# Second layer of a graph network: two maxima of the next tile between the two weight products of this one, on Vector

## The chip, the cores and the metric

The kernel runs on one core of one Trainium2 chip. The metric is the time of one execution on the device, in microseconds; of several runs the median is given. The profile comes from one further execution.

## The reference

Two message-passing layers over 6250 nodes and 200000 edges, each with a residual and a layer norm. The change concerns the second layer only. For each edge e with 16 attributes and source node features h (16), it computes two 16 x 16 matrices and a softmax over the edges of a destination node:

```
w_m = (efeat @ W_msg + b_msg).reshape(E, 16, 16)
w_a = (efeat @ W_attn + b_attn).reshape(E, 16, 16)
e1 = w_m * feat[src][:, :, None]
e2 = w_a * feat[src][:, :, None]
seg_max = segment_max(e2, dst)
ex = exp(e2 - seg_max[dst])
attn = ex / segment_sum(ex, dst)[dst]
ft = segment_sum(e1 * attn, dst)
out = layernorm(x + x + ft.sum(axis=1))      # second x: the layer's input again
```

The last line is shortened to what matters: the layer adds its messages to its input and normalises.

## The kernel before, in words

The edges are sorted by destination. The first layer and all tables are made ahead, up to about 3000 us into the span; the second layer's loop over its edges follows, and a last block gathers the sums by node and normalises, from about 6095 us on. Only the loop is of interest here (kernel lines 1007 to 1298).

The loop runs over NT = 214 tiles. A tile is 128 partitions (lanes) times J = 8 edges, in two groups of G4 = 4; all edges of a group have the same destination. A lane walks along its sorted edges, so the running maximum and the running sums are carried from group to group and from tile to tile in the tiles `state` and `ps`. A device loop (`rounds`, L1024) has eight tiles in its body, since buffers rotate by tile number: `work`, `xg` and `state` have four buffers each, PSUM's `pw` has four banks.

In one step of the loop each engine works on the tile `now` and on its neighbours, in its own written order; semaphores join the engines.

- GpSimd gathers the source features of a later tile, eight indirect DMAs (L1082), and the edge rows of a still later one (L1091). The eight gathers wait until Vector has finished with the buffer.
- TensorE (L1152 on) sums the four edges of the previous tile's first group into PSUM (L1172, eight passes in f32), turns the edge rows of the next tile but one (L1195), waits for ScalarE's L1116 and for the second weight product, sums three edges of the second group (L1172), makes half of the difference of maxima (L1207, L1181), and makes the next tile's weights, 99 x 512 per edge (`weigh`, L1166), into `pw`.
- Vector (L1223 on) is where the change is. In a step it does, before the change: `maxima(now)`: two 512-wide maxima over pairs of edges, L1248 for the first group and L1250 for the second (each waits for ScalarE's masks, the semaphore `masked`), both into `top`; L1252, a maximum of these; three 256-wide scalar_tensor_tensor that carry the maximum from the tile before (L1254, L1258, L1261); two subtractions (L1266), one per group. Then the four L1235 of `edges(ahead)`: weights times source features, from `pw` into `work`, each of which waits for TensorE. Then L1281 of `carry_on(now)`, which scales the carried sums, and two products `products(now, half)` (L1273): exponentials times messages, one per group, each after ScalarE's exponential. Instructions that need the result of the one just before them on Vector wait for it through the semaphore `chain`; it rises by MS = 5 per tile.
- ScalarE (L1096 on) multiplies one edge's weights itself (L1109), fills and copies sums (L1116, L1117, L1148), turns rows to bf16 (L1123), takes two exponentials per tile (L1129), one of the difference (L1131), and masks the eight edges of the next tile (L1141), two after each of Vector's L1235.
- SP stores `state` for each tile (L1050, L1052) and loads the next metadata (L1040).

The order of each engine's work is the order in which these lines are written; no planner moves it.

The functions that the diff touches, and what calls them:

Of the kernel before, what the change touches and what calls it, by code (L numbers as in the profile page):

```python
# [52 lines left out]
C = D * D  # L53
# [42 lines left out]
def gnn(nc, x, src, dst, ea16, ea8, node_vec1, Wmt, Wml, Wut, Wul, Wm, bm, Wa, ba, out):  # L96
    ctx = ExitStack()
    with ctx:
# [96 lines left out]
        with ExitStack() as st:  # L195
            def tsb(name, shape, dt=F32):
                return st.enter_context(nc.sbuf_tensor(name, shape, dt))
# [16 lines left out]
            first = tsb("first", [PL, TN + 1])  # L214
# [748 lines left out]
        with ExitStack() as st:  # L963
# [8 lines left out]
            state = tsb("state", [GP, 4, 6 * C])  # L972
            top = tsb("top1", [GP, 7, C])
# [36 lines left out]
            def tile(t, q, off):  # L1010

                m = q + off
                if isinstance(t, int) and not 0 <= U * t + m < NT:
                    return None
                return U * t + m, m % U, t + m // U

            def channels(t, a=None):
                return t.rearrange("p (i o) -> p i o", i=D) if a is None else t.rearrange("p (i a o) -> p i a o", i=D, a=a)

            def wait(eng, what, value):  # L1020
                if not isinstance(value, int) or value > 0:
                    eng.wait_ge(what, value)

            def rounds(eng, body, before, after):  # L1024

                for n in range(-before, U):
                    body(n // U, n % U)
                with eng.Fori(1, NT // U) as t:
                    for q in range(U):
                        body(t, q)  # L1030
                for n in range(NT // U * U, NT + after):
                    body(n // U, n % U)

            def word(b, i):
                return mt[:, b, i:i + 1].bitcast(F32)
# [187 lines left out]
            @block.vector  # L1223
            def _(v):
                v.sem_inc(w_used, 2)
                v.tensor_scalar(nident[:, :], ident[:, :], -1.0, None, ALU.mult)
                v.wait_ge(primed, 1)
                v.wait_ge(ps_zeroed, 1)

                def edges(at, i):  # L1230

                    n, b, r = at
                    v.wait_ge(w_made, J * n + i + 2)
                    k = 1 if i == 2 else 2
                    v.tensor_tensor(work[:, b % 4, i:i + k, :, :, :].rearrange("p j i a o -> p (j i) (a o)"),  # L1235
                                    pw[:, i % 4:i % 4 + k, :].rearrange("p j (i c) -> p (j i) c", i=D),
                                    xg[:, b % 4, i:i + k, :].rearrange("p j i -> p (j i)").unsqueeze(2).to_broadcast([GP, k * D, 2 * D]),
                                    ALU.mult).then_inc(w_used, 1)

                def maxima(at):  # L1240

                    n, b, r = at
                    s = work[:, b % 4, :, :, 0, :]
                    out = lambda lo, hi: top[:, lo:hi, :].rearrange("p j (i o) -> p j i o", i=D)
                    both = top[:, 0:4, :].rearrange("p (g s) c -> p g s c", g=2)
                    before, first, second = state[:, (b - 1) % 4, C:2 * C], state[:, b % 4, 0:C], state[:, b % 4, C:2 * C]
                    v.wait_ge(masked, J * n + G4)
                    v.tensor_tensor(out(0, 2), s[:, 0:2], s[:, 2:4], ALU.max)  # L1248
                    v.wait_ge(masked, J * n + J)
                    v.tensor_tensor(out(2, 4), s[:, 4:6], s[:, 6:8], ALU.max).then_inc(chain, 1)  # L1250
                    v.wait_ge(chain, MS * n + 1)
                    v.tensor_tensor(top[:, 4:6, :], both[:, :, 0, :], both[:, :, 1, :], ALU.max).then_inc(chain, 1)  # L1252
                    v.wait_ge(chain, MS * n + 2)
                    v.scalar_tensor_tensor(out=top[:, 6, :], in0=before, scalar=word(b, FIRST_NEG),  # L1254
                                           in1=top[:, 4, :], op0=ALU.add, op1=ALU.max).then_inc(chain, 1)
                    wait(v, stored[b % 4], 32 * (2 * r + b // 4))
                    v.wait_ge(chain, MS * n + 3)
                    v.scalar_tensor_tensor(out=second, in0=top[:, 6, :], scalar=word(b, SECOND_NEG),  # L1258
                                           in1=top[:, 5, :], op0=ALU.add, op1=ALU.max).then_inc(chain, 1)
                    v.wait_ge(chain, MS * n + 4)  # L1260
                    v.scalar_tensor_tensor(out=first, in0=second, scalar=word(b, SECOND_NEG),  # L1261
                                           in1=top[:, 6, :], op0=ALU.add, op1=ALU.max).then_inc(chain, 1)
                    v.wait_ge(chain, MS * n + 5)
                    for half, most in enumerate((first, second)):
                        s = work[:, b % 4, half * H:(half + 1) * H, :, 0, :]
                        v.tensor_tensor(s, s, channels(most).unsqueeze(1).to_broadcast([GP, H, D, D]),  # L1266
                                        ALU.subtract).then_inc(less, 1)

                def products(at, half):
                    n, b, r = at  # L1270
                    v.wait_ge(exped, 2 * n + half + 1)
                    w = work[:, b % 4, half * H:(half + 1) * H, :, :, :]
                    v.tensor_tensor(w[:, :, :, 1, :], w[:, :, :, 1, :], w[:, :, :, 0, :], ALU.mult).then_inc(p_done, 2)  # L1273

                def carry_on(at):

                    n, b, r = at
                    v.wait_ge(corr_done, n + 1)
                    wait(v, b_summed, n)
                    wait(v, a_copied, n)  # L1280
                    v.tensor_tensor(channels(ps[:, 0, :], 2), channels(ps[:, 1, :], 2),  # L1281
                                    channels(corr[:, b % 4, :]).unsqueeze(2).to_broadcast([GP, D, 2, D]),
                                    ALU.mult).then_inc(carried, 1)

                def body(t, q):
                    now, ahead = tile(t, q, 0), tile(t, q, 1)
                    if now:
                        maxima(now)
                    if ahead:
                        v.wait_ge(x_in[ahead[1] % 4], 16 * J * (2 * ahead[2] + ahead[1] // 4 + 1))  # L1290
                        for i in range(0, J, 2):
                            edges(ahead, i)
                    if now:
                        carry_on(now)
                        for half in range(2):
                            products(now, half)

                rounds(v, body, 1, 0)


        with ExitStack() as st:
# [4 lines left out]
            both = tsb("both", [GP, 2, 2 * C])  # L1306
# [4 lines left out]
            top = tsb("top", [128, 4, 2 * GP])  # L1311
# [303 lines left out]
```

## Time and profile before

| | us |
|---|---|
| median of 3 runs | 6270.4 (6248.13 to 6270.71) |
| profiled execution, own time | 6239.89 |
| its span, first to last instruction | 6238.2 |
| Vector busy | 4702.9 (75%) |
| TensorE matmul busy | 4599.3 (74%) |
| GpSimd busy | 4058.2 (65%) |
| ScalarE busy | 3051.0 (49%) |

The span is that of the program's instructions; the execution's own time is a little more. Busy shares are averages over the whole span, both layers together. A duration is that of one instruction; on Vector two neighbours can overlap by about 0.09 us, so distances between starts tell more than durations. Ends of matmuls are modelled. A line with a `[0.31 <-X]` had that much idle time of its engine before it, ended by X; "issue" stands for nothing that the profile shows, "remote" for a semaphore that rose with no instruction of the trace beside it.

### The profile page before, as it was taken

To read this page: it belongs to the slowest core of one execution; us is meant where nothing else is said; L and a number is where in the kernel's file an instruction comes from. 1 tells how busy PE (TensorE), PEld (TensorE's weight loads), DVE (VectorE), ACT (ScalarE), POOL (GpSimd) and SP (SyncE) were. 2 spreads that over 40 slices of the span, in tenths; PEclk is the share of its full clock that TensorE was granted. 3 is DMA by queue.
4 is the path that set the end of the run, shared out by engine and by line. 5 is a ranking of instruction groups with operands and counts; after the bars stand their busy time and mean duration, and the time that the engine had idled before them with its cause. 6 is when DMAs were issued, how large, how long until landed. Compare 5 with 4: busy or idle time off the path is not lost. (4 is left out here: it accounts for less than half of the span.)

```text
span 6238.2 us, 73171 instructions
## 1 busy us (share of the span) xinstructions
PE 4599.3 (74%) x17323; PEld 2095.9 (34%) x17471; DVE 4702.9 (75%) x7634; ACT 3051.0 (49%) x7980; POOL 4058.2 (65%) x3679
## 2 busy tenths in 40 slices
PE   2367777767677777778588888888888888888881
PEld 1133333333333333334233333333333333333330
DVE  5565666756566566666598988898889989889996
ACT  1121212212122222221387777777777877777783
POOL 5666666666666566663577777777777777777754
PEclk5677787877887787887699999999999999999995
DMA  4222222222222222221122222222222222222224
GB/s 131 64 61 62 60 63 60 65 61 60 62 62 60 58 64 61 62 60 37 32 81 75 77 76 76 71 76 76 75 75 76 76 76 76 76 76 76 76 68 116
DMA packets 350921, 435.22 MB, mean 70 GB/s; under 512 B 172480, under 2 KB 252747, under 8 KB 350509
## 3 DMA queue, kind: packets, MB, share of 16 engines
q1 hardware_dynamic: 222605, 246.69, 12.5%
q0 software_dynamic: 128160, 187.16, 12.0%
q14 instruction: 145, 1.19, 0.1%
q8 instruction: 11, 0.18, 0.0%
HBM read 214.10 MB, written 219.29 MB: 69 GB/s over the span
## 5 line engine op out<-in xcount | busy, mean ns | idle before, releaser
L1082 POOL DMA_INDIRECT xg<-x1tab,edge x1712 | 1977.8, 1155 | 780.3 <-issue 549.8
L628 POOL DMA_INDIRECT bg<-btab,mt x1568 | 1700.1, 1084 | 995.6 <-DMA e<-in_edge_attr_dram 522.1
L830 PE MATMUL pagg<-ohh,stt 128*128 128x512 bf16 x4557 | 1752.5, 418 | 393.9 <-issue 368.7
L1172 PE MATMUL ps<-work,ident 128*128 128x512 f32 x3424 | 1737.3, 643 | 209.8 <-ACT ps L1116 99.8
L831 PE MATMUL pagg<-ohh,stt 128*128 128x270 bf16 x4704 | 1416.6, 301 | 359.9 <-issue 341.3
L1235 DVE TENSOR_TENSOR work<-pw,xg 128x1024 f32<-128x1024 f32 x856 | 911.5, 1087 | 311.8 <-PE pw L1166 167.1
L787 ACT CAST joined<-rest 128x256 bf16<-128x256 f32 x196 | 79.7, 407 | 2108.8 <-DVE rest L713 1433.5
L1172 PEld LDWEIGHTS ps<-work,ident 128*128 128x128 f32 x3424 | 664.3, 205 | 950.9 <-issue 867.6
L830 PEld LDWEIGHTS pagg<-ohh,stt 128*128 128x128 bf16 x4704 | 485.0, 103 | 1142.2 <-issue 675.9
L740 DVE TENSOR_TENSOR res<-sact,s 128x128 f32<-128x128 f32 x196 | 56.7, 289 | 976.7 <-remote 830.9
L1141 ACT ACTIVATE work<-work,mt 128x256 f32<-128x256 f32 x1712 | 737.0, 498 | 107.6 <-DVE work L1235 67.3
L1166 PE MATMUL pw<-w,et 99*128 99x512 bf16 x1712 | 540.0, 398 | 333.6 <-DVE work L1235 180.6
L831 PEld LDWEIGHTS pagg<-ohh,stt 128*128 128x128 bf16 x4704 | 481.3, 102 | 622.9 <-issue 521.5
L1109 ACT ACTIVATE work<-pw,xg 128x32 f32<-128x32 f32 x3424 | 632.4, 337 | 98.4 <-issue 66.4
L743 DVE TENSOR_SCALAR ohh<-iota_hi,hilo 128x782 bf16<-128x782 f16 x1568 | 637.6, 428 | 0.0
L1266 DVE TENSOR_TENSOR work<-work,state 128x1024 f32<-128x1024 f32 x428 | 505.3, 1222 | 7.4
L1273 DVE TENSOR_TENSOR work<-work 128x1024 f32<-128x1024 f32 x428 | 503.1, 1217 | 0.0
L1129 ACT ACTIVATE work<-work 128x1024 f32<-128x1024 f32 x428 | 439.9, 1066 | 8.5 <-DVE work L1266 1.0
L758 DVE TENSOR_TENSOR stt<-s,ohx 128x1024 bf16<-128x1024 bf16 x588 | 400.7, 682 | 0.0
L1166 PEld LDWEIGHTS pw<-w,et 99*128 99x128 bf16 x1712 | 123.5, 98 | 732.9 <-issue 414.5
L728 DVE TENSOR_REDUCE msg<-bg 128x128 f32<-128x1024 f32 x196 | 365.2, 1863 | 0.0
L1116 ACT ACTIVATE ps<-ps,mt 128x512 f32<-128x512 f32 x214 | 143.9, 672 | 372.4 <-issue 206.0
(269 smaller groups left out, 4204.2 us busy)
## 6 DMA issues: line engine op xcount, KB each, us to landing
ssum<-state SPq DMA_DIRECT2D x214, 512.0 KB
smax<-state SPq DMA_DIRECT2D x214, 256.0 KB
etab<-joined SPq DMA_DIRECT2D x389, 102.0 KB
xg<-x1tab,edge POOLq DMA_INDIRECT x1712
bg<-btab,mt POOLq DMA_INDIRECT x1568
e<-in_edge_attr_dram SPq DMA_DIRECT2D x392, 32.0 KB
e<-in_edge_attr_dram SPq DMA_DIRECT2D x392, 16.0 KB
btab<-bst SPq DMA_DIRECT2D x7, 512.0 KB
```

The lines of the kernel that those rows point to most:

```text
L628: g.indirect_dma_start(bg[:, h, i, :], None, btab, bass.IndirectOffsetOnAxis(ap=mt[:, h, 0, i:i + 1], axis=0)).then_inc(gathered[h], 16)
L743: v.tensor_scalar(ohh[:, h, i, :], iota_hi[0:LANES, :], hilo[:, h, 0, i:i + 1], None, ALU.is_equal).then_inc(ohh_done, 1)
L830: pe.matmul(pagg[:, 0, :], w, ohh[:, h, i, 0:CUT], start=False, stop=False, skip_group_check=True)
L831: ins = pe.matmul(pagg[:, 1, 0:HI - CUT], w, ohh[:, h, i, CUT:HI], start=False, stop=False, skip_group_check=True)
L1082: g.indirect_dma_start(xg[:, b % 4, i, :], None, x1tab, bass.IndirectOffsetOnAxis(ap=edge[:, b, i, EW - 1:EW], axis=0)).then_inc(x_in[b % ...
L1109: ins = act.activation(work[:, b % 4, 3, c, :, :].rearrange("p a o -> p (a o)"), pw[:, 3, 2 * D * c:2 * D * (c + 1)], ACT.Identity, scale= ...
L1141: act.activation(s, s, ACT.Identity, bias=word(b, MASKS + i)).then_inc(masked, 1)
L1166: pe.matmul(pw[:, i % 4, :], et[:, b % 2, i, :], w99[:, :], start=True, stop=True).then_inc(w_made, 1)
L1172: return pe.matmul(ps[:, i // G4, :], ident[:, :], work[:, b % 4, i, :, :, :].rearrange("p i a o -> p (i a o)"), start=False, stop=i % G4 ...
L1235: v.tensor_tensor(work[:, b % 4, i:i + k, :, :, :].rearrange("p j i a o -> p (j i) (a o)"), pw[:, i % 4:i % 4 + k, :].rearrange("p j (i c) ...
L1266: v.tensor_tensor(s, s, channels(most).unsqueeze(1).to_broadcast([GP, H, D, D]), ALU.subtract).then_inc(less, 1)
L1273: v.tensor_tensor(w[:, :, :, 1, :], w[:, :, :, 1, :], w[:, :, :, 0, :], ALU.mult).then_inc(p_done, 2)
```

## The change

`maxima` is cut in two. Its first two instructions, L1248 and L1250, become `first_maxima`, with their waits for the masks and the rise of `chain` on the second. The rest keeps the name. On Vector `first_maxima` is called for the tile `ahead`, between the two products of the tile `now`; the rest of `maxima` comes at the start of the next step, as before. No instruction is added or removed, and none on another engine is moved.

```
-                def maxima(at):
+                def first_maxima(at):
 
                     n, b, r = at
                     s = work[:, b % 4, :, :, 0, :]
                     out = lambda lo, hi: top[:, lo:hi, :].rearrange("p j (i o) -> p j i o", i=D)
-                    both = top[:, 0:4, :].rearrange("p (g s) c -> p g s c", g=2)
-                    before, first, second = state[:, (b - 1) % 4, C:2 * C], state[:, b % 4, 0:C], state[:, b % 4, C:2 * C]
                     v.wait_ge(masked, J * n + G4)
                     v.tensor_tensor(out(0, 2), s[:, 0:2], s[:, 2:4], ALU.max)
                     v.wait_ge(masked, J * n + J)
                     v.tensor_tensor(out(2, 4), s[:, 4:6], s[:, 6:8], ALU.max).then_inc(chain, 1)
+
+                def maxima(at):
+
+                    n, b, r = at
+                    both = top[:, 0:4, :].rearrange("p (g s) c -> p g s c", g=2)
+                    before, first, second = state[:, (b - 1) % 4, C:2 * C], state[:, b % 4, 0:C], state[:, b % 4, C:2 * C]
                     v.wait_ge(chain, MS * n + 1)
                     v.tensor_tensor(top[:, 4:6, :], both[:, :, 0, :], both[:, :, 1, :], ALU.max).then_inc(chain, 1)
...
                     if now:
                         carry_on(now)
-                        for half in range(2):
-                            products(now, half)
+                        products(now, 0)
+                    if ahead:
+                        first_maxima(ahead)
+                    if now:
+                        products(now, 1)
```

## Rows read from the trace of the kernel before

**Rows 1.** Page, busy tenths in 40 slices of the span.

```profile
PE   2367777767677777778588888888888888888881
...
DVE  5565666756566566666598988898889989889996
...
PEclk5677787877887787887699999999999999999995
```

**Rows 2.** Vector's timeline, one dense tile: start, duration, engine, line, tiles, count.

```profile
4024.29 2.35 DVE L1273 TENSOR_TENSOR work<-work 128x1024 f32<-128x1024 f32 x2
4026.56 0.69 DVE L1248 TENSOR_TENSOR top<-work 128x512 f32<-128x512 f32 x1
4027.16 0.68 DVE L1250 TENSOR_TENSOR top<-work 128x512 f32<-128x512 f32 x1
4027.88 0.69 DVE L1252 TENSOR_TENSOR top<-top 128x512 f32<-128x512 f32 x1
...
4037.41 1.22 DVE L1273 TENSOR_TENSOR work<-work 128x1024 f32<-128x1024 f32 x1
```

**Rows 3.** Vector's timeline: first and last first product of the 212.

```profile
3104.36 2.35 DVE L1273 TENSOR_TENSOR work<-work 128x1024 f32<-128x1024 f32 x2
...
6091.93 2.35 DVE L1273 TENSOR_TENSOR work<-work 128x1024 f32<-128x1024 f32 x2
```

**Rows 4.** Vector's waits for others from 3104 to 6092: us, times, longest.

```profile
DVE work L1235 <- PE pw L1166: 140.0, 91, 4.5
DVE work L1235 <- issue: 51.0, 40, 3.0
DVE work L1235 <- remote: 44.9, 25, 4.5
```

**Rows 5.** Vector's groups by form, 3104 to 6092; last: idle before, us.

```profile
L1252 DVE TENSOR_TENSOR top<-top 128x512 f32<-128x512 f32 x211 | 146.0, 692 | 7.3
```

**Rows 6.** Vector's timeline of a 14.26 us tile.

```profile
3996.91 2.35 DVE L1273 TENSOR_TENSOR work<-work 128x1024 f32<-128x1024 f32 x2
...
4008.13 2.52 DVE L1235 TENSOR_TENSOR work<-pw,xg 128x1024 f32<-128x1024 f32 x2 [1.24 <-PE pw L1166]
...
4011.17 1.22 DVE L1273 TENSOR_TENSOR work<-work 128x1024 f32<-128x1024 f32 x1
```

**Rows 7.** TensorE's timeline in the tile of rows 6.

```profile
3998.18 5.40 PE L1172 MATMUL ps<-work,ident 128*128 128x512 f32 x8 [0.35 <-DVE work L1273]
```

**Rows 8.** Vector's timeline of a 16.20 us tile.

```profile
4040.28 0.68 DVE L1250 TENSOR_TENSOR top<-work 128x512 f32<-128x512 f32 x1
...
4050.36 1.22 DVE L1235 TENSOR_TENSOR work<-pw,xg 128x1024 f32<-128x1024 f32 x1 [2.97 <-remote]
...
4053.61 1.22 DVE L1273 TENSOR_TENSOR work<-work 128x1024 f32<-128x1024 f32 x1
```

**Rows 9.** TensorE's timeline of the dense tile of rows 2.

```profile
4025.65 3.67 PE L1172 MATMUL ps<-work,ident 128*128 128x512 f32 x8 [0.45 <-DVE work L1273]
...
4030.17 2.81 PE L1172 MATMUL ps<-work,ident 128*128 128x512 f32 x6 [0.40 <-ACT ps L1116]
...
4033.73 0.60 PE L1166 MATMUL pw<-w,et 99*128 99x512 bf16 x2 [0.32 <-issue]
...
4035.03 1.23 PE L1166 MATMUL pw<-w,et 99*128 99x512 bf16 x4
```

**Rows 10.** Dense tile, whole loop: PE, PEld, DVE, ACT, POOL busy; clock, DMA.

```profile
4024.29:4037.41 13.12, 11.17 (x37) 4.68 (x36) 12.77 (x17) 11.29 (x33) 10.22 (x9) 1.00 0.27 82
3104.36:6091.90 2987.54, 2487.37 (x7569) 1049.68 (x7568) 2689.84 (x3162) 2350.56 (x6517) 2115.07 (x1860) 0.94 0.25 75
```

**Rows 11.** ScalarE's timeline around the last two masks.

```profile
4036.93 0.91 ACT L1141 ACTIVATE work<-work,mt 128x256 f32<-128x256 f32 x2 [0.39 <-issue]
```

**Rows 12.** GpSimd's timeline: a gather in a dense tile, one after a late tile.

```profile
4024.55 1.77 POOL L1082 DMA_INDIRECT xg<-x1tab,edge  x1 [0.45 <-issue]
...
4053.87 1.77 POOL L1082 DMA_INDIRECT xg<-x1tab,edge  x1 [3.54 <-DVE work L1235]
```

## Prediction

> **What bounds the kernel now.** I read the page first. The change touches only the loop over the 214 tiles of the second layer, so the first question is what sets the length of one tile there. In the page's slices Vector is at 8 or 9 tenths through the right half of the span and TensorE at 8 [rows 1]. Neither is clearly alone at the top, so a view by tile is needed.
>
> The second view is Vector's timeline of one tile [rows 2]. I measure a tile from the start of its first weight product (L1273) to the start of the next tile's. The reader should see that in this tile, 4024.29 to 4037.41, each instruction starts when the one before it is hardly done: 13.12 us, no idle time named anywhere. Here Vector is the bound, and a tenth of a microsecond saved on it is a tenth of the tile.
>
> The third view tells how often this is so. The 212 first products of the settled loop start between 3104.36 and 6091.93 [rows 3], so 211 tiles take 2987.57 us, a mean of 14.16 and not 13.12. Sorted by the distance of their starts, 87 of the 211 take 13.2 us or less (mean 13.11), 22 take 13.2 to 13.6, 58 take 13.6 to 15 (mean 14.40) and 44 take 15 to 17.4 (mean 16.31). Over 13.12 apiece the 124 longer tiles hold 220 us. The list of Vector's waits says where: 156 waits of L1235 (91, 40 and 25), 236 us together, all for TensorE's pw or with no releaser named [rows 4]. Two tiles show it: one of 14.26 us with 1.24 idle before the third L1235 [rows 6], one of 16.20 us, 4037.41 to 4053.61, with 2.97 [rows 8].
>
> So there are two kinds of tile. In 87 Vector is the bound. In 124 TensorE hands the next tile's weights over late, and Vector waits for it. What makes TensorE late can be seen in part: in the 14.26 us tile the eight passes of L1172 take 5.40 us, in the 13.12 us tile 3.67 [rows 7, 9]. The granted clock over the loop is 0.94 of 2.4 GHz, in the dense tile 1.00, so part of the time is spent at the 1.2 GHz level [rows 10].
>
> **The change, part by part.** The number and shapes of instructions stay the same. L1248 and L1250 of the next tile move up by one product, and the second product moves down by two maxima.
>
> *The wait between L1250 and L1252.* L1252 reads what L1250 wrote and waits for it. In [rows 2] L1248 to L1250, which have no such wait, start 0.60 us apart (4026.56, 4027.16); L1250 to L1252, with nearly the same duration, start 0.72 apart (4027.16, 4027.88). The wait costs 0.12 us: 0.09 of overlap of two neighbours and some 0.03 of idle, which the groups give as 7.3 us over 211 L1252 [rows 5]. After the change the second product stands between them. Its 1.13 us (half of the 2.27 from L1273 to L1248) covers the wait. The other pairs keep their distances: the product needs no result of L1250, so 0.60 again, and L1252 needs none of the product, so 1.13 again. The dense tile becomes 1.13 + 0.60 + 0.60 + 1.13 in place of 1.13 + 1.13 + 0.60 + 0.72, that is 3.46 for 3.58, or 13.00 us for 13.12.
>
> *In how many tiles this counts.* TensorE's chain through a tile starts at the end of the first product (L1172 at 4025.65 [rows 9]) and hands back at the third and fourth L1235; Vector then does L1281 and the next first product. Neither the second product nor a maximum stands on that way. So in a tile where Vector waits for TensorE it arrives 0.12 earlier and waits 0.12 longer. I take 87 tiles: 87 x 0.12 = 10 us. The bounds are 0 (the distance stays 0.72 for a reason other than the wait) and 214 x 0.12 = 26 us (TensorE's lateness moves along with Vector). I take 10, since the late tiles' waits of 1.24 and 2.97 us are far above 0.12. For the 87 to get it in full TensorE must be ready for the earlier first L1235: it sat idle 0.32 us before L1166 at 4033.73 [rows 9], which is over 0.12.
>
> *The masks are needed 1.13 us earlier.* L1250 waits for the eighth mask of the next tile (L1141 on ScalarE). The last two begin at 4036.93 and end at 4037.84 [rows 11]. The old L1250 starts at 4040.28 [rows 8], the new one would at 4039.14 (4037.41 + 1.13 + 0.60), so 1.30 us of cover are left. Both ends hang on the fourth L1235, so this distance holds in late tiles too. Cost nothing. Were the cover gone, Vector itself would stand, and with it the second product, which is queued behind L1250.
>
> *The second product ends 1.20 us later.* TensorE's last four sums and their L1172 wait for it. It would end at 4024.29 + 2.33 + 1.22 = 4027.84; TensorE begins that group at 4030.17, released by ScalarE's L1116 [rows 9], so 2.3 us are left. Cost nothing. If that went, L1166 would come late by the difference.
>
> *GpSimd.* A gather takes 1.77 us beside Vector's products, and 1.1 in the mean over a dense tile (10.22 us for nine) [rows 10, 12]. The change leaves the set of Vector instructions as it is and gathers run beside all of them, so I take the same stretching. The eight gathers and the L1091 need 10.2 us [rows 10] plus nine gaps of at least 0.30, so 12.9: under 13.00, closely (one is 0.45 today [rows 12], which would make it 13.07; were that its least, GpSimd would hold dense tiles there once its lead is used up). They run more than two tiles ahead (L1082 at 4053.87 waits for Vector, not the other way [rows 12]), and the mean tile is 14.16. Cost nothing; no DMA is moved in any queue, and SP's stores wait for ScalarE's L1148, which the change does not touch.
>
> *A rule against the change.* The row shows 0.72 with a wait and 0.60 without [rows 2]. The Trainium skill, "VectorE: DVE Perf Modes", section "The DRAIN you can't avoid", says that a semaphore after each Vector instruction costs nothing more than one at the end of the chain: the next does not start before the pipe is empty either way. By that rule the sum is 0, and it is rival 1 below; this trace disagrees with it by 0.12 us, as the instructions without a wait overlap by 0.09.
>
> **The sum.** 10 us less of the profiled execution's own 6239.9 (span 6238.2) is 6230. The median of the three runs shown is 6270.4, 30 above that execution; 10 less is 6260. I state 6260.
>
> **The rivals.**
> 1. *No gain.* The distance from L1250 onwards doesn't shrink, as some other bound takes the place of the wait: 0 us, 6270. For it: of the 0.12 only 0.03 shows as idle [rows 5], the rest is overlap, and the row can't tell what allows it. Against: 0.60 and 0.72 are for equal shapes. 11%.
> 2. *The whole loop gains.* 214 x 0.12 = 26 us, 6244. For it: nothing but that Vector is 90% busy (2690 of 2988 us [rows 10]). Against: the waits of [rows 6, 8], which are for TensorE. 12%.
> 3. *Fewer late tiles.* 102 tiles of over 13.6 us hold 215 us, 2.1 each. A dense tile of 13.00 us puts TensorE's thin stretch (from the end of the L1166 at 4035.03 until the next L1172, some 2.5 us with four short matmuls [rows 9]) elsewhere against the clock's falls. How often these hit is then open. With 15 fewer late tiles: 10 + 32 = 42, 6229. For it: less idle before L1166 per tile. 20%.
> 4. *More late tiles*, the other side. The same mechanism, place and price with the other sign: after a thin stretch L1172 runs at 1.2 GHz (5.40 for 3.67 us [rows 7, 9]) and the third L1235 waits. Five more late tiles eat the 10 us; with 25 more, 52 - 10 = 42 slower, 6312. For it: dense tiles follow each other in runs of one to three before a late one, and shorter ones may meet the fall in as many microseconds but more often per tile. Against: the work between two falls stays the same. 12%.
>
> **How the numbers follow.** The forecast has 45%. Bounds of the known costs are 0 to 26 us, that is 6244 to 6270; the runs of before alone spread over 22 us. Taking in rival 3's centre and half of rival 4's way gives 6225 to 6290, which leaves out rival 4's centre and the far ends of both. What a measurement of this kernel tells from no change is 0.5%, or 31 us. Faster by more than that takes rival 3, and a little of the rest is lost to its near end: 20%. Slower by more takes rival 4: 11%, the near end of it being within 0.5%. Within 0.5% is the rest, 69%.
>
> **What would show it.** Dense tiles at 13.00 us on Vector, with the moved L1248 1.13 after the first product, the moved L1250 0.60 after that, the second product 0.60 after it and the third maximum 1.13 after the product, would bear out the 0.12. No new wait before the moved pair would bear out the mask's cover, and an unchanged start of TensorE's second group of L1172 that of the product. Late tiles of unchanged length would bear out the count. The prediction is wrong if the number of late tiles moves by over ten, or if the moved L1250's line shows a wait for ScalarE.

## The result, and the profile after

| | before | changed |
|---|---|---|
| median of four runs each | 6267.5 us (6248.13 to 6270.71) | 6223.2 us (6209.73 to 6224.39) |
| ratio, 95% interval | | 0.9931, 0.9915 to 0.9948 |
| profiled execution's span | 6238.2 | 6222.7 |
| 211 settled tiles of the second layer | 2987.6 | 2966.7 |

The change made the kernel 43 us faster in this comparison; 10 had been forecast, and the measured time lies 2 us below the range. The profile of before was a quick execution of that kernel, so the spans differ by 16 only. Later comparisons give another picture: with the same two kernels the gain was 25 us in one session, and in two others the changed kernel was slower by 20 and 33 (all by the ratios; the medians themselves differ by 44, 20, 24 and 34). A session here is one set of runs side by side on one chip; the kernel before itself took 6250, 6040 and 5470 us in different ones. So two questions need an answer: where the forecast 10 us are, and what puts a larger amount of either sign on top of them.

Vector's timeline of a dense tile of the changed kernel, from first product to first product, is the first view (start, duration, engine, line, tiles). The product is now L1277, the two first maxima L1246 and L1248, the third L1256.

```profile
4002.91 1.21 DVE L1277 TENSOR_TENSOR work<-work 128x1024 f32<-128x1024 f32 x1
4004.04 0.68 DVE L1246 TENSOR_TENSOR top<-work 128x512 f32<-128x512 f32 x1
4004.65 0.68 DVE L1248 TENSOR_TENSOR top<-work 128x512 f32<-128x512 f32 x1
4005.25 1.26 DVE L1277 TENSOR_TENSOR work<-work 128x1024 f32<-128x1024 f32 x1
4006.43 0.68 DVE L1256 TENSOR_TENSOR top<-top 128x512 f32<-128x512 f32 x1
...
4015.95 1.21 DVE L1277 TENSOR_TENSOR work<-work 128x1024 f32<-128x1024 f32 x1
```

The starts stand 1.13, 0.61, 0.60 and 1.18 apart, 3.52 in sum, where the kernel before has 3.59 between the same points [rows 2]. The wait is covered as forecast, but the second product now takes 1.26 us instead of 1.22 and holds up L1256 by 0.05. The dense tile is 13.04 us, not 13.00, and the saving 0.08 to 0.09, not 0.12.

ScalarE's masks and TensorE's second group of sums, in the same tile of the changed kernel:

```profile
4015.47 0.91 ACT L1141 ACTIVATE work<-work,mt 128x256 f32<-128x256 f32 x2 [0.39 <-DVE work L1235]
```

```profile
4008.72 2.81 PE L1172 MATMUL ps<-work,ident 128*128 128x512 f32 x6 [0.40 <-ACT ps L1116]
...
4012.27 0.60 PE L1166 MATMUL pw<-w,et 99*128 99x512 bf16 x2 [0.30 <-issue]
```

The last mask ends at 4016.38, and the moved L1248 that needs it starts at 4017.68: the 1.30 us of cover are there. TensorE's group is still released by ScalarE, 5.8 us after the first product's start where it was 5.9 [rows 2, 9]. Vector's waits over the settled loop of the changed kernel (us, times, longest) say the same and show the rest:

```profile
DVE work L1235 <- PE pw L1166: 148.1, 88, 5.5
DVE work L1235 <- issue: 56.6, 44, 2.0
DVE work L1235 <- remote: 27.5, 9, 4.5
...
DVE top L1248 <- ACT work L1141: 0.5, 2, 0.3
```

There are 141 waits of L1235 in place of 156 [rows 4], 232 us in place of 236; the moved maximum waits for ScalarE twice in these 211 tiles. Sorted by length as in the prediction, 90 tiles take up to 13.2 us, 22 up to 13.6, 66 up to 15 and 33 more. That is 121 longer tiles for 124, but 33 over 15 us for 44. Dense tiles give back 90 x 0.08 = 7 us of the 21 by which the loop is shorter; 14 lie in the late ones.

### The profile page after: what moved, and what is told of

Same layout as the page of the kernel before. It is cut to its first block and busy times, and to the rows that moved or that the text cites. A ratio compares the mean times of both kernels' runs of the same rounds, so it can differ in the third digit from the quotient of the medians.

```text
span 6222.7 us, 73121 instructions
## 1 busy us (share of the span) xinstructions
PE 4615.3 (74%) x17323; PEld 2099.6 (34%) x17471; DVE 4690.8 (75%) x7634; ACT 3048.5 (49%) x7980; POOL 4041.5 (65%) x3679
## 5 line engine op out<-in xcount | busy, mean ns | idle before, releaser
L1172 PE MATMUL ps<-work,ident 128*128 128x512 f32 x3424 | 1754.3, 648 | 224.2 <-ACT ps L1116 90.1
L1235 DVE TENSOR_TENSOR work<-pw,xg 128x1024 f32<-128x1024 f32 x856 | 910.6, 1086 | 297.0 <-PE pw L1166 154.8
L1172 PEld LDWEIGHTS ps<-work,ident 128*128 128x128 f32 x3424 | 668.6, 206 | 970.5 <-issue 852.4
L1166 PE MATMUL pw<-w,et 99*128 99x512 bf16 x1712 | 526.6, 390 | 285.3 <-DVE work L1235 170.1
L1277 DVE TENSOR_TENSOR work<-work 128x1024 f32<-128x1024 f32 x428 | 528.2, 1234 | 0.0
```

Source lines behind the costliest of these rows:

```text
L1166: pe.matmul(pw[:, i % 4, :], et[:, b % 2, i, :], w99[:, :], start=True, stop=True).then_inc(w_made, 1)
L1172: return pe.matmul(ps[:, i // G4, :], ident[:, :], work[:, b % 4, i, :, :, :].rearrange("p i a o -> p (i a o)"), start=False, stop=i % G4 ...
```

## The experiments

Seven sessions; "before" is the kernel before, run in the same session. Only sessions 1 and 4 have a profile of it, so where late tiles are counted against it, the counts are often of two sessions. Sessions 2 to 7 ran on chips that the record numbers 0, 13, 5, 11, 6 and 0: number 0 stands for 6040 us once and for 5470 the other time. "Pad N" is a memset of 128 x N on Vector behind the second product, "matmuls added" is explained with e6. Late is a tile over 0.5 us longer than that kernel's dense ones, counted from the start times of the first product in the profile, over 211 tiles; in brackets those over 1.9 longer. The loop is the sum of the 211. For e11 and e12, the light kernels, the column "dense" has the most frequent length.

| session, before | kernel | time | ratio (interval) | dense | late | loop |
|---|---|---|---|---|---|---|
| 1, 6267.5 | changed | 6223.2 | 0.9931 (0.9915 to 0.9948) | 13.04 | 103 (35) | 2967 |
| | before | | | 13.12 | 102 (44) | 2988 |
| 2, 6039.7 | e1 one between | 6026.1 | 0.9969 (0.9942 to 0.9996) | 13.12 | 53 (7) | 2841 |
| | e2 pad 16 | 6048.7 | 1.0000 (0.9976 to 1.0023) | 13.05 | 79 (7) | 2861 |
| 3, 6252.6 | e5 changed | 6232.4 | 0.9960 (0.9934 to 0.9986) | 13.04 | 103 (35) | 2973 |
| | e6 before, matmuls added | 6325.1 | 1.0105 (1.0072 to 1.0139) | 13.12 | 116 (82) | 3094 |
| | e7 changed, matmuls added | 6299.0 | 1.0066 (1.0044 to 1.0088) | 13.04 | 123 (80) | 3050 |
| | e8 pad 80 | 6232.1 | 0.9967 (0.9940 to 0.9994) | 13.07 | 100 (38) | 2983 |
| 4, 5469.8 | e9 before again | 5468.7 | 0.9997 (0.9988 to 1.0006) | 13.12 | 42 (0) | 2821 |
| | e10 pad 512 | 5529.3 | 1.0106 (1.0090 to 1.0122) | 13.60 | 14 (0) | 2878 |
| | e11 light before | 5441.1 | 0.9944 (0.9926 to 0.9962) | 13.39 | 0 | 2796 |
| | e12 light changed | 5421.2 | 0.9904 (0.9886 to 0.9923) | 13.30 | 1 | 2775 |
| 5, 6039.5 | e13 short before | 6142.2 | 1.0185 (1.0160 to 1.0209) | 12.86 | 108 (41) | 2937 |
| | e14 changed | 6063.6 | 1.0033 (1.0010 to 1.0056) | 13.04 | 84 (6) | 2865 |
| | e15 pad 512 | 6067.6 | 1.0048 (1.0027 to 1.0068) | 13.60 | 13 (0) | 2878 |
| 6, 5465.2 | e16 pad 256 | 5526.6 | 1.0113 (1.0099 to 1.0126) | 13.33 | 67 (0) | 2880 |
| | e17 pad 384 | 5526.9 | 1.0111 (1.0098 to 1.0124) | 13.46 | 44 (0) | 2878 |
| | e18 changed | 5499.7 | 1.0061 (1.0048 to 1.0074) | 13.04 | 79 (1) | 2851 |
| 7, 5470.2 | e19 changed, matmuls added | 5414.1 | 0.9892 (0.9872 to 0.9911) | 13.04 | 9 (0) | 2761 |
| | e20 before, matmuls added | 5427.5 | 0.9916 (0.9898 to 0.9933) | 13.12 | 1 (0) | 2775 |

**Length or place (e1, e2).** Theory A says the gain hangs on the length of Vector's tile, theory B on the new place of product and maxima. In e1 only one maximum stands between:

```
                    if now:
                        carry_on(now)
                        products(now, 0)
                    if ahead:
                        first_maxima(ahead, 0)
                    if now:
                        products(now, 1)
                    if ahead:
                        first_maxima(ahead, 1)
```

> Only the first group's maximum (L1248 before) stands between the two products; the second group's follows the second product, so the next maximum still stands right behind the one whose result it needs and its wait stays uncovered. The second product ends 0.60 us later than in the kernel before instead of 1.20. Theory A (length: what counts is how long a tile is on Vector, through the covered wait): dense tiles as before, 13.12 us or up to 0.04 more as products and maxima alternate once more; time as before, 6250 to 6275 us. Theory B (place: the later second product or the earlier maximum itself makes TensorE late less often): about half of the gain or more, 6220 to 6250 us.

e2 adds to the changed kernel, behind the second product:

```
+                        v.memset(pad[:, 0:16], 0.0)
```

> The changed kernel with one tiny memset (128 x 16) on Vector behind the second product of each tile, which gives back roughly the 0.08 us per dense tile that the change saved (13.04 up to about 13.10 to 13.15 us). Theory A (length): the gain goes as a whole, both the direct 7 to 10 us and the rest, and the time is again 6245 to 6275 us. Theory B (place): only the direct part goes, 6223 + 7 to 10 = 6228 to 6236 us. If the number of late tiles answers to the length in no simple way, the time can also come out on the other side of before.

e1 has the wait and 13.12 us, as A says, and came out 0.3% faster, hardly clear of none. e2 gained nothing against before, though its tile is only 0.015 longer than the changed one. Neither theory had expected that; without the changed kernel beside them it was not to be read.

**The changed kernel again, a larger pad, and matmuls added (e5 to e8).** e8 is e2 with `pad[:, 0:80]`. e6 adds to the kernel before, and e7 to the changed one, nine matmuls whose result nobody reads. They write over `pt`; in a first form (e3, e4) they had a PSUM tensor of their own, for which PSUM had no room, and gave no result.

```
+            unread = pt[:, :, :].rearrange("p j c -> p (j c)").bitcast(F32)
...
+                def keep_busy(times):
+                    for _ in range(times):
+                        pe.matmul(unread[:, 0:256], identb[0:KS, :], w99[:, 0:256], start=True, stop=True)
...
                         pe.wait_ge(carried, n + 1)
+                        keep_busy(4)
                         for i in range(G4):
...
                         for i in range(4):
+                            if i == 2:
+                                keep_busy(5)
                             weigh(next_but_one, i)
```

> The changed kernel once more, beside the kernel before on the same chip, as the chip of the first experiments ran the kernel before in 6040 and not in 6268 us and with fewer late tiles (63 in the profile of the kernel with one maximum between). Theory A in its direct part (0.08 us in each dense tile, some 120 to 150 of 211 there): 10 to 12 us less than the kernel before, ratio 0.998. If the 43 us of the first pair belong to the change itself (theory B, or A with its pattern of late tiles), the ratio is 0.993 here too.

> The kernel before with nine added bf16 matmuls of 256 columns per tile on TensorE, whose result nobody reads, in the two stretches in which it waits for Vector (five before the third weight of the next tile but one, four before the sums of the first group). Theory A says that late tiles come from TensorE at the 1.2 GHz level after such thin stretches: with them filled the granted clock of the loop goes to 0.98 or more, late tiles mostly vanish, and 211 tiles take near 211 x 13.12 = 2768 us, 70 to 220 us less than the kernel before on that chip. The rival (TensorE is late for another reason, as in tiles of over 15 us whose matmuls start at full pace): the clock rises but those tiles stay; or the added matmuls delay TensorE, slower than before.

> The same nine added matmuls in the changed kernel. If late tiles vanish in both, the change is worth its 0.08 us (13.12 to 13.04) in each of 214 tiles: 17 us less than the kernel before with added matmuls, and no more. Theory B (place) expects more than 25 us between the two, as the place would help beside the clock. If the added matmuls don't reach the late tiles, the two differ by about what the kernels without them do on that chip.

> The changed kernel with a memset of 128 x 80 on Vector behind the second product; the one of 128 x 16 added only 0.015 us to a dense tile (13.05), this one should bring it to 13.10 to 13.14, the length of before. Theory A (length): same time as the kernel before within 6 us on the same chip. Theory B (place): still faster than the kernel before by most of what the changed kernel is.

The changed kernel gained 0.4%, 9 to 41 us by the interval: between both figures of the expectation. e8 gave back 0.03 of the 0.085 us per tile and its time didn't move, so A is not decided by it. In e6 the late tiles did not vanish. Those between 0.5 and 1.9 us over are 34, against 58 in session 1, but those over 1.9 are 82, against 44, and the time rose by 66 us. The two profiles of one session, e5 and e7, say the same of the changed kernel: 68 to 43, and 35 to 80. So there are two kinds of late tile, and the second gets more frequent with more TensorE work.

**Slope, and less work on TensorE (e9 to e12).** e10 adds a memset of 128 x 512 to the kernel before, behind the second product. In e11 and e12 only edges 0 and 4 are summed:

```
-                        for i in range(G4):
-                            if i % 2 == 0:
-                                pe.wait_ge(p_done, H * n + i // 2 + 1)
-                            ins = total(done, i)
-                        ins.then_inc(a_summed, 1)
+                        pe.wait_ge(p_done, H * n + 2)
+                        total(done, 0).then_inc(a_summed, 1)
...
-                        total(done, 4)
-                        total(done, 5)
-                        total(done, 6)
+                        total(done, 4).then_inc(b_summed, 1)
...
-                    if done:
-                        total(done, 7).then_inc(b_summed, 1)
```

> The kernel before, unchanged, timed against itself, for the scatter of a ratio and for a second profile of it. Both theories: ratio 1.000 with an interval of some 0.0025 to either side, dense tiles of 13.12 us, about 220 us over 211 x 13.12 if the chip is like the first.

> The kernel before with a memset of 128 x 512 on Vector behind the second product of every tile, off TensorE's way just as the second product and the maxima are. It makes a dense tile longer by x (read from the profile; 0.3 to 0.6 us expected, so 13.4 to 13.7). Accounting of the prediction: late tiles absorb it, since Vector waits for TensorE in them, so the whole costs 90 x plus little, 54 us at x = 0.6. Rival (the loop as a whole moves with Vector's length, as the time lost to TensorE stays the same in sum): 211 x, 127 us at x = 0.6.

> The kernel before without six of the eight sums of each tile on TensorE (edges 1 to 3 of the first group, 5 to 7 of the second are left out of the sums; the second group's one sum stands where its first one stood). TensorE has 5.2 us less per tile, so it should hardly ever be late even at its 1.2 GHz level: 211 tiles of 13.12 to 13.3 us, 2768 to 2806 in place of 2988.

> The changed kernel with the same six sums left out. With TensorE out of the way the two must differ by what the change saves on Vector alone: 0.08 to 0.09 x 214 = 17 to 19 us, both theories of length. If a place effect exists that doesn't need TensorE (gathers on GpSimd beside other instructions), the difference is larger than 25 us.

Session 4 ran the kernel before in 5470 us with 42 late tiles, the longest of 14.34 us; sessions like it are called quiet below. e9 against itself gives 0.9997 within 0.0009. e12 is 20 us under e11, and its loop 21, that is 0.10 us per tile: about what the change saves on Vector, with no room for a large effect of the place. But TensorE is not out of the way in these two. Left with so little work it runs at a granted clock of 0.71, and Vector still waits for it 154 times in the loop of e11 (79 us) and 148 times in that of e12 (76 us), which is why their most frequent tile is 13.39 and 13.30 us. These waits did not grow by what Vector saved, for TensorE itself waits there for Vector's L1228 (L1235 of before) to free the place of the weights, so the whole round is tied to Vector:

```profile
3505.95 1.89 PE L1166 MATMUL pw<-w,et 99*128 99x512 bf16 x4 [2.83 <-DVE work L1228]
```

The cleaner pair for the direct part comes with e19 and e20. e10 costs 60 us for 0.48 us per tile, 57 of them in the loop, where letting the 42 late tiles absorb what they can gives 76: it has 14 late tiles for 42. The number of late tiles isn't fixed. It moves with Vector's length. Their own length does not: the late tiles of e10 take up to 14.33 us, those of e9 up to 14.34.

**Shorter, the same, longer, in one session (e13 to e15).** e13:

```
-                    v.tensor_tensor(out(0, 2), s[:, 0:2], s[:, 2:4], ALU.max)
+                    v.tensor_tensor(out(0, 1), s[:, 0:1], s[:, 2:3], ALU.max)
...
-                    v.tensor_tensor(top[:, 4:6, :], both[:, :, 0, :], both[:, :, 1, :], ALU.max).then_inc(chain, 1)
+                    v.tensor_tensor(top[:, 4:6, :], top[:, 2:4, :], top[:, 2:4, :], ALU.max).then_inc(chain, 1)
```

> The kernel before with the first maximum of a tile (L1248) at half its width, 256 in place of 512 elements, which takes about 0.27 us off every tile on Vector, off TensorE's way. It leaves half of the first group's edges out of the maximum, and the next maximum reads the second group's result twice. Accounting of the prediction: late tiles keep their length, so 0.27 x dense tiles: 24 us less with 90 dense tiles, 41 with 150. Rival (the whole loop moves with Vector's length): 0.27 x 214 = 58 us less on any chip.

> The changed kernel on the same chip. Accounting of the prediction: 0.08 to 0.09 us x dense tiles, 8 us less with 90, 13 with 150. Rival: 18 us less on any chip. More than 25 us less would be an effect of its own beside Vector's length.

> The kernel before with the memset of 128 x 512 (0.48 us more per tile). Accounting of the prediction, late tiles counted one by one: 43 us more with 90 dense tiles, 73 to 77 with 150, less what falls away where late tiles become fewer (59.5 us measured where the kernel before takes 5470 us). Rival: 103 us more on any chip.

All expectations of sign for the first two fell. With 0.27 us less on Vector the kernel is 103 us slower by the medians, with 0.085 less 24 slower. Their late tiles number 108 and 84, against 53 at 13.12 us in a session of the same time (e1) and 13 at 13.60. What dense tiles gain is lost several times over. The tiles over 1.9 us late number 41 in e13 and 6 in e14, in one session: the second kind answers to Vector's length too, not only to TensorE's work.

**Two lengths between, and the changed kernel (e16 to e18).** As e10, with 256 and 384 columns.

> The kernel before with a memset of 128 x 256 on Vector per tile, about 0.2 us more (dense 13.3). Smooth dependence: the time over 211 dense lengths falls from 70 to about 30 us on a chip where the kernel before takes 6040 us (net 0, within 10 us of before), from 220 to about 100 on one where it takes 6250 (80 us faster), from 53 to 25 on one of 5470 (15 slower). Accounting of the prediction (number of late tiles fixed): 20 to 30 us slower on any. Chance pattern: either sign.

> The same with 128 x 384, about 0.35 us more (dense 13.45). Smooth dependence: over 211 dense lengths some 15 us are left on the 6040 us chip (net 10 to 15 slower than before), 50 on the 6250 one (100 faster). Accounting of the prediction: 35 to 50 us slower on any chip.

> The changed kernel on the same chip: on a chip of the 6250 kind 20 to 40 us faster than before, on one of the 6040 kind 10 to 25 slower, on one of the 5470 kind 5 to 15 faster (152 of 211 tiles dense there, at 0.085 us, less what more late tiles take).

The count is not smooth in the length: 79 late tiles at 13.04, 42 at 13.12 (e9), 67 at 13.33, 44 at 13.46, 14 at 13.60. The order in which late tiles come tells more. Late tiles in e18 are every second tile eight or nine times over, then seven dense ones follow, then eight or nine late ones again, through the whole loop. In e16 mostly every third is late, in e17 every fourth or fifth, in e10 every twelfth (twelve to fifteen apart); at 13.12 us (e9) they come irregularly, with stretches of 7 to 18 dense tiles. TensorE's timeline in a dense and the next, late tile of e18:

```profile
3504.84 3.67 PE L1172 MATMUL ps<-work,ident 128*128 128x512 f32 x8 [0.45 <-DVE work L1277]
...
3514.14 1.23 PE L1166 MATMUL pw<-w,et 99*128 99x512 bf16 x4
3516.05 0.60 PE L1166 MATMUL pw<-w,et 99*128 99x512 bf16 x2 [0.69 <-DVE work L1235]
3516.73 0.69 PE L1181 MATMUL gap<-state,ident 128*128 128x256 f32 x2
3517.87 5.34 PE L1172 MATMUL ps<-work,ident 128*128 128x512 f32 x8 [0.44 <-DVE work L1277]
...
3532.16 3.67 PE L1172 MATMUL ps<-work,ident 128*128 128x512 f32 x8 [0.44 <-DVE work L1277]
```

The late tile's eight passes take 5.34 us, part of them at 1.2 GHz, right behind the thin stretch from 3515.4; the dense ones 3.67. Vector's third L1235 then waits 1.36 us, and the tile takes 14.29. This is [rows 6, 7] of before.

The traces also hold the times at which the granted clock falls to 1.2 GHz, and these settle what the first kind of late tile is. The loops of e10, e9, e17, e16 and e18 have 15, 40, 45, 68 and 79 falls, for 14, 42, 44, 67 and 79 late tiles. All but one per loop, in its last tile, begin in a late tile, 1.28 to 1.64 us after its first product, about where L1172 starts, and every late tile of about 14.3 us has one. In e18 the stretch from 3517.80 to 3521.20 us has a granted clock of 0.50, and the rest of that tile 1.00.

**The thin stretch filled, in a quiet session (e19, e20).** The kernels of e7 and e6.

> The changed kernel with the nine added bf16 matmuls of 256 columns per tile in TensorE's two thin stretches. On a chip where the kernel before takes 5470 us and no tile is over 15 us: if the thin stretches cause the falls of the clock, the tiles of 14.3 us go from 78 to under 10 and the loop to 211 x 13.04 = 2751 us, some 70 us less than that of the kernel before and 100 less than that of the changed one (5500 to 5400). If not, no change in their number, or slower through the matmuls. On a chip of the 6250 kind: 40 to 50 us slower than before again; on one of 6040: between.

> The same in the kernel before. If the falls go, the two differ by Vector's saving in all tiles, 211 x 0.085 = 18 us, and the kernel before with the matmuls stands at 5418 on the 5470 kind. If the falls stay, the difference is set by their numbers again and may have either sign.

Vector's waits for TensorE in the loops of e9 (before), e18 (changed) and e19 (changed, matmuls added), one fence each:

```profile
DVE work L1235 <- PE pw L1166: 59.1, 59, 1.3
```

```profile
DVE work L1235 <- PE pw L1166: 109.7, 79, 2.2
```

```profile
DVE work L1243 <- PE pw L1171: 13.5, 24, 0.8
```

And the loops of the same three as one stretch each (busy PE, PEld, DVE, ACT, POOL; granted clock, DMA share, GB/s); that of e19 begins 7 us before its loop and ends 17 us before the loop's end:

```profile
2499.60:5320.90 2821.30, 2412.01 (x7569) 1014.86 (x7568) 2691.01 (x3163) 2361.07 (x6517) 2138.39 (x1879) 0.98 0.27 80
```

```profile
2501.00:5351.90 2850.90, 2474.41 (x7569) 1040.43 (x7568) 2679.26 (x3163) 2351.19 (x6517) 2123.36 (x1880) 0.95 0.27 79
```

```profile
2499.00:5250.00 2751.00, 2537.68 (x9448) 1168.68 (x9448) 2671.34 (x3151) 2365.35 (x6513) 2127.53 (x1884) 1.00 0.28 82
```

The changed kernel has a lower clock than the kernel before, 0.95 for 0.98 of 2.4 GHz, 20 more waits and 51 us more in them. With TensorE's thin stretches filled the clock stays at 1.00, with one fall in the whole loop of e19 and one in that of e20; nine late tiles are left in e19, each under 0.7 us over, and the changed kernel is the faster one, 5414 to 5427. This pair shows the direct part: dense tiles of 13.04 and 13.12 us, and loops of 2761 and 2775, 14 us apart where 211 x 0.085 is 18; most of the rest is in the nine late tiles. In session 7 the changed kernel with the added matmuls is 1% under the kernel before; the changed kernel without them was not run beside it, and stands above the kernel before in the like session 6. It is no general winner, though: as e7 the same kernel is 0.7% slower than before in session 3.

## Why the prediction was right or wrong

*The wait's 0.12 us.* Right in kind: it goes. Two maxima start 0.60 us apart without the wait and 0.72 with it, and the kernels differ by 13 us between e19 and e20. The Trainium skill, "VectorE: DVE Perf Modes", section "The DRAIN you can't avoid", says that the semaphore costs nothing extra, measured with tensor_copy; these rows and this pair disagree. The same section says that a next instruction that is not held starts earlier, and with that the 0.60 agrees. The size was 0.085, for the product behind two maxima takes 1.26 us; with a single maximum before it, in e1, it takes 1.22.

*Masks, second product, GpSimd at nothing.* Right. The cover of 1.30 us and the unchanged start of TensorE's second group stand in the profile after, the moved maximum waited for ScalarE twice, 0.5 us in all, and the gathers of a dense tile still take from 0.94 to 1.77 us each.

*"In a tile where Vector waits for TensorE it arrives 0.12 earlier and waits 0.12 longer."* For a tile with one fall of the clock this holds: such tiles last 14.24 to 14.34 us at every length of Vector's from 13.04 to 13.60 (e18, e9, e16, e17, e10). But the sum took the longer tiles as fixed in number and kind, 87 dense and 124 longer, and so put their change at nothing. That step failed. It was named as rivals 3 and 4, with 20 and 12% and opposite signs, and measured larger than the direct part: from 42 late tiles (e9) to 79 (e18) in sessions of 5470 us. Over 211 of its own dense tiles the loop holds 53 us in e9 and 101 in e18, so +48, against -18 for 211 tiles of 0.085. The sum, +30, is the loop's 2851 less 2821; the kernel's medians differ by 34 in session 6.

*In the first comparison* the number of late tiles was the same, 102 and 103, and their time over the own dense length too: 2988 - 211 x 13.12 = 219 us before, 2967 - 211 x 13.04 = 216 after. In e5 it is 222. So there the whole loop is shorter by 211 x 0.085 = 18 us and 3 more, where 10 had been summed: dense tiles give 7 as said, and 14 come from the late ones, which the prediction had put at nothing. The figure is rival 2's at the measured 0.085, but its mechanism, a saving in each tile, is not shown by that: the tiles over 1.9 us late went from 44 to 35 and held 140 and 127 us, those below went from 58 to 67 and held 74 and 83. That the sum comes out like this may be chance. Of the 43 us the loop is under half. The rest is in no part of the two profiles, whose spans differ by 16, and one kernel's runs scatter as much: 27 runs of before in session 3 span 68 us. The first four runs against four gave more than the 25 us (9 to 41) of e5; that this is scatter is likely and not shown. Why the number stays at 102 in such sessions and doubles in others is not settled.

*What stays open.* Tiles over 15 us, 44 in the first profile [rows 8], were as good as absent in sessions 4, 6 and 7 (one, of 15.13 us, in e18). In the tile of [rows 8] TensorE's transposes and weights, and ScalarE's copy of the transposed rows, stand like this:

```profile
4042.28 0.61 PE L1195 MATMUL pt<-identb,edge 128*99 128x128 bf16 x8
...
4045.32 1.01 ACT L1123 COPY et<-pt 99x1024 bf16<-99x1024 bf16 x1 [1.67 <-remote]
...
4046.85 0.61 PE L1166 MATMUL pw<-w,et 99*128 99x512 bf16 x2 [0.32 <-DVE work L1235]
```

The transposes are recorded as done at 4042.89, and the copy waits until 4045.32; the weights as done at 4047.46, and Vector waits for them until 4050.36 [rows 8]. The granted clock from 4046.85 to 4050.36 is 1.00, so this wait is no fall. A fall often comes behind it, once TensorE has stood idle: of the 44 such tiles 30 have the full clock through their first 12 us, 39 have a fall begin after that, and 30 of these are followed by a late tile. So the second kind brings part of the first. More TensorE work made it more frequent (35 in e5, 80 in e7), and so did a shorter tile on Vector (6 in e14, 41 in e13). What makes it, and why sessions differ, no run here shows. That the thin stretch brings the falls is shown for the sessions of 5470 us (79 falls in e18, one in e19 in the next session); that the length of a tile picks their rhythm is shown by the regular spacing, not derived.

## What to carry to other kernels

Before you sum a saving over the tiles in which an engine is the bound, ask whether the other tiles come late by a rhythm of their own: read the sequence of tile lengths, not only their sorted counts. If every second or third tile waits behind a TensorE at 1.2 GHz, a tenth of a microsecond on another engine can shift that pattern by more than it saves, as 0.085 us did here in two sessions. Try such an edit with TensorE's thin stretch filled as well, as in e19 and e20, to see what it saves by itself; whether the filling pays depends on the session (5470 to 5427 us in one, 6253 to 6325 in another). And compare in more than one session.

## What the runs showed of the hardware that was not expected

- The kernel before took 5470, 6040 and 6250 us in different sessions, with intervals of a tenth to a quarter of a percent inside each. The part ahead of the settled loop differs as well: it begins at 3104 us in session 1 [rows 3] and at 2500 in session 4.
- With 0.27 us less work per tile on Vector the kernel was 1.85% slower (e13).
- With six of eight sums left out TensorE's granted clock over the loop was 0.71, with a fall in nearly every tile, and the loop was yet the shortest without added matmuls (e12, 2775 us).
- Late tiles with one fall of the clock take 14.24 to 14.34 us, whether Vector's own tile is 13.04 or 13.60 us long (e18, e10).
- A memset of 128 x 80 takes 0.12 us and lengthened the tile by only 0.03, as the next maximum starts 0.04 us after it and takes 0.62 in place of 0.68 (e8).
